# Graph-attention kernel: the normalised adjacency built inside the attention's last batch, and small buffers placed behind the large ones

## The reference

```python
# layer 0, per batch: attention with 4 heads whose queries come from a weighted adjacency product
A = abs(abs(sigmoid(diff) - 0.5) - 0.5) * 2.0
g = relu(einsum('bcn,bnm->bcm', fea, adj * (A + A.T) / 2) * para)
attn = softmax(einsum('bhnd,bhmd->bhnm', q, k) * scale);  out = attn @ v
x = layernorm(x + out)
# layer 1: graph convolution with the normalised adjacency, two linear layers with batch norms
A_norm = adj + eye(n)
deg = A_norm.sum(0) + A_norm.sum(1) - diagonal(A_norm)
dinv = rsqrt(deg)
A_hat = A_norm * dinv[:, None] * dinv[None, :]
agg = einsum('nm,bmd->bnd', A_hat, x)
h = relu(batchnorm(agg @ W1.T + b1));  out = batchnorm(h @ W2.T + b2)
x = layernorm(x + out)
```

## Time and profile before

| | us |
|---|---|
| median of 3 runs (lowest to highest) | 2815.95 (2815.73 to 2816.79) |
| the profiled execution's own time | 2817.06 |
| its span, first to last instruction | 2815.0 |
| TensorE busy | 2680.3 (95%) |
| VectorE busy | 1996.8 (71%) |
| ScalarE busy | 1662.9 (59%) |
| GpSimd busy | 1297.0 (46%) |

### The profile page before, as it was taken

The page is one execution under the profiler, slowest core; times in us unless marked ns, Lnnn a source line. Parts: engine busy times, 40 slices in busy tenths (PEclk is TensorE's granted clock), DMA queues, the critical chain, the costliest instruction groups (busy, mean ns, idle before and its releaser), DMA issues. The chain is left out here.

```text
span 2815.0 us, 39437 instructions
## 1 busy us (share of the span) xinstructions
PE 2680.3 (95%) x12436; PEld 1860.1 (66%) x12436; DVE 1996.8 (71%) x2875; ACT 1662.9 (59%) x2159; POOL 1297.0 (46%) x687
## 2 busy tenths in 40 slices
PE   8999999999999999999999999996899999989964
PEld 6566675656656566565666756663688888878854
DVE  7788796877868778797887968773533333348878
ACT  7666676675767667676666766754222222237768
POOL 5755757556575664757547575564100000000025
PEclk9999999999999999999999999998999999999985
DMA  4232222332222322223322223212122233215566
GB/s 139 77 96 75 75 78 75 92 95 75 67 86 69 102 90 67 71 78 97 93 72 75 78 75 97 75 53 105 60 90 89 104 104 104 90 32 192 180 242 250
DMA packets 126943, 272.01 MB, mean 97 GB/s; under 512 B 11952, under 2 KB 62128, under 8 KB 123312
## 3 DMA queue, kind: packets, MB, share of 16 engines
q1 hardware_dynamic: 126896, 271.42, 29.9%
HBM read 178.79 MB, written 62.98 MB: 86 GB/s over the span
## 5 line engine op out<-in xcount | busy, mean ns | idle before, releaser
L305 POOL TENSOR_TENSOR psum<-psum,probs 128x1024 f32<-128x1024 f32 x320 | 785.2, 2454 | 131.7 <-ACT probs L391 105.5
L391 ACT ACTIVATE probs<-sc_ps 128x1024 f32<-128x1024 f32 x512 | 507.6, 1023 | 403.2 <-PE sc_ps L852 400.2
L580 DVE TENSOR_REDUCE mx<-mx_ps 128x1 f32<-128x512 f32 x768 | 524.3, 690 | 255.2 <-PE mx_ps L821 252.6
L868 PE MATMUL pv_ps<-probs,v 128*64 128x512 f32 x2048 | 492.4, 604 | 0.0
L852 PE MATMUL sc_ps<-qa,ka 128*128 128x512 f32 x1024 | 387.3, 404 | 0.0
L852 PE MATMUL sc_ps<-qb,kb 128*128 128x512 f32 x1024 | 380.9, 395 | 1.6 <-DMA qb<-row 1.2
L821 PE MATMUL mx_ps<-ka,qa 128*128 128x512 f32 x768 | 314.2, 416 | 11.1 <-DVE mx L580 8.2
L868 PEld LDWEIGHTS pv_ps<-probs,v 128*64 128x64 f32 x2048 | 125.6, 136 | 220.8 <-issue 184.2
L1202 DVE TENSOR_TENSOR agg_lo<-ag_ps,agg_hi 128x1024 fp32r<-128x1024 f32 x32 | 39.2, 1224 | 312.3 <-ACT agg_hi L1129 312.3
L852 PEld LDWEIGHTS sc_ps<-qa,ka 128*128 128x128 f32 x1024 | 187.5, 188 | 106.9 <-issue 77.1
L821 PEld LDWEIGHTS mx_ps<-ka,qa 128*128 128x128 f32 x768 | 142.2, 187 | 161.6 <-issue 78.7
(11 more groups left out here) (198 smaller groups left out, 5524.5 us busy)
## 6 DMA issues: line engine op xcount, KB each, us to landing
adj_ring<-in_adj_dram SPq DMA_DIRECT2D x128, 512.0 KB, 3.6
pre_scratch<-pre SPq DMA_DIRECT2D x28, 1024.0 KB, 4.5
pre<-pre_scratch SPq DMA_DIRECT2D x28, 1024.0 KB, 5.0
x<-in_x_dram SPq DMA_DIRECT2D x16, 1024.0 KB, 5.5
kb<-ka SPq DMA_DIRECT2D x64, 256.0 KB, 3.2
res<-in_x_dram SPq DMA_DIRECT2D x16, 1024.0 KB, 5.5
x_scratch<-res SPq DMA_DIRECT2D x16, 1024.0 KB, 4.5
x1s<-x_scratch SPq DMA_DIRECT2D x16, 1024.0 KB, 7.5
```

The lines of the kernel that those rows point to most:

```text
L305: pool.tensor_tensor(psum[:, h % 2, :], probs[:, 0, :] if k == 1 else psum[:, h % 2, :], probs[:, k % PR, :], ALU.add).then_inc(s["pool_ad ...
L391: nc.scalar.activation(probs[:, i % PR, :], sc_ps[:, t % 2, :], ACT.Exp, scale=SCALE)\
L580: nc.vector.tensor_reduce(mx2[:, nh, n:n + 1], mx_ps[:, nh, :], AX.X, ALU.max)\
L868: ins = nc.tensor.matmul(pv_ps[nh * HD:(nh + 1) * HD, h % 2, :], v[:, i, h * HD:(h + 1) * HD], probs[:, i % PR, nh * BANK:(nh + 1) * BANK] ...
```

## The change

Part 1. The adjacency is made in the last batch of the attention. Its buffers `a_hi` and `a_lo` (and `pre`, `w2_hi`, `w2_lo`) are now made ahead of the attention, whose own buffers lie inside them as long as they are needed (`x32`, `neg_para` and `probs` in `pre`; `w_hi`, `x_hi`, `xT_hi`, `ka[0]` in `a_hi`). The slabs of `adj` are loaded in the last batch (SP), VectorE adds the identity and takes the diagonal after head 1's row (`augment`), ScalarE takes row sums in heads 2 and 3, TensorE the column sums in head 3 (`column_sums`), GpSimd `dinv` between its adds of head 3. ScalarE scales five slabs by `dinv`, VectorE three; TensorE transposes, ScalarE writes `a_hi` and VectorE `a_lo`, scaling by the other `dinv` on the way.

Part 2. `aggregate_layer` starts with the load of batch 0 in four pieces; the first product starts when the first piece is split, and the weights are transposed in its middle.

Part 3. `neg_half_b` and `neg_half_c` stand behind the large buffers. By the sizes, `a_hi`, `x1_hi`, `w1_hi`, `agg_hi`, `hid_hi` and their low parts all start on a multiple of 64 bytes now, as `w2_hi` does. In the attention `probs`, `ka[0]` and `qa[0]` start on one, while `v`, `kb`, `qb` and the other `ka` and `qa` are 32 bytes past.

Part 4. The last batch's result is normalised and stored in two halves.

```diff
+            def load_slabs(k):
+                if k == 0:
...
+                for t in SLABS[k]:
+                    sp.dma_start(slabs[t], slab_v[t]).then_inc(slabs_in[k], 16)
...
+            for k in range(2):
+                rows = slice(T // 2 * k, T // 2 * (k + 1))
+                wait(sp, s["res_done"], B + k)
+                sp.dma_start(x1_v[B - 1][:, rows, :], res[:, rows, :]).then_inc(s["x1_out"], 16)
...
+                        if last and (h, k) == (3, 1):
+                            pool.wait_ge(s["deg_done"], 1)
+                            pool.wait_ge(s["pool_added"], done + 1)
+                            pool.tensor_tensor(dinv[:, :], deg[:, :], neg_half[:, :], ALU.pow)\
+                                .then_inc(s["dinv_done"], 1)
...
+            def normal_adjacency(h, p):
+
+                if h == 2:
+                    for t in ((0,), (1, 2), (3, 4), (5, 6))[p]:
+                        row_sum(t)
+                if (h, p) == (3, 0):
+                    row_sum(7)
+                    col_copy()
+                if (h, p) == (3, 1):
+                    for t in ACT_SLABS[0:3]:
+                        scale_slab(t)
+                if (h, p) == (3, 2):
+                    for t in ACT_SLABS[3:]:
+                        scale_slab(t)
...
+            a_high(0)
             head_copy(B - 1, HEADS - 1)
+            a_high(1)
             den_copy(B - 1, HEADS - 1)
-            normalise(B - 1)
+            for m in range(2, 5):
+                a_high(m)
+            normalise(B - 1, range(0, T // 2))
+            normalise(B - 1, range(T // 2, T))
+            for m in range(5, T):
+                a_high(m)
...
+                    if h == 1 and last:
+                        augment(0)
+                        augment(1)
+                    if h == 2 and last:
+                        diagonal()
...
+                if last:
+                    degrees()
+                    scale_slabs(DVE_SLABS[0:2])
                 invert_sums(b, 2)
+                if last:
+                    scale_slabs(DVE_SLABS[2:])
...
+            a_low(0)
             add_last(B - 1, HEADS - 1)
+            a_low(1)
             invert_sums(B - 1, HEADS - 1)
             add_head(B - 1, HEADS - 1)
             row_stats(B - 1)
             moments(B - 1)
+            for m in range(2, T):
+                a_low(m)
...
+            def column_sums():
+                pe.wait_ge(s["augmented"], T)
+                pe.wait_ge(s["row_done"], 4 * B)
+                for t in range(T):
+                    for g in range(4):
+                        ins = nc.tensor.matmul(mx_ps[g * SG:(g + 1) * SG, 0, 0:SN], ones[:, :],
+                                               slabs[t][:, g * SN:(g + 1) * SN], start=t == 0, stop=t == T - 1)
+                ins.then_inc(s["colsum_ready"], 1)
...
+            def transpose_adjacency(m):
+                if m == 0:
+                    pe.wait_ge(s["scaled_act"], len(ACT_SLABS))
+                    pe.wait_ge(s["scaled_dve"], len(DVE_SLABS))
+                    pe.wait_ge(s["deg_done"], 1)
+                if m == 1:
+                    pe.wait_ge(s["exp_done"], 32 * B)
+                wait(pe, s["atl_done"], m - 2)
+                for t in range(T):
+                    ins = nc.tensor.transpose(at_tile(m)[:, t * P:(t + 1) * P], slabs[t][:, m * P:(m + 1) * P], ident[:, :])
+                ins.then_inc(s["at_ready"], 1)
...
-        neg_half = sb("neg_half_b", [P, T])
-        a_hi = sb("a_hi", [P, T, N], F32R)
-        a_lo = sb("a_lo", [P, T, N], F32R)
...
+        neg_half = sb("neg_half_b", [P, HT])
...
+            for k in range(PIECES):
+                rows = slice(PT * k, PT * (k + 1))
+                dve.wait_ge(piece_in[k], 16)
+                nc.vector.tensor_copy(x1_hi[:, rows, :], x1s[:, 0, rows, :]).then_inc(s["first_high"], 1)
+                dve.wait_ge(s["first_high"], k + 1)
+                nc.vector.tensor_tensor(x1_lo[:, rows, :], x1s[:, 0, rows, :], x1_hi[:, rows, :].bitcast(F32),
+                                        ALU.subtract).then_inc(s["first_low"], 1)
...
                 for m in range(T):
...
+                    pe.wait_ge(s["first_low"], m // PT + 1)
+                    if m == T // 2:
+                        transpose_weights()
...
-        neg_half = sb("neg_half_c", [P, OT])
         hid_hi = sb("hid_hi", [P, HT, N], F32R)
         hid_lo = sb("hid_lo", [P, HT, N], F32R)
...
+        neg_half = sb("neg_half_c", [P, OT])
```

More of the change, by code:

```diff
@@ L52, in row_moments, with attention_layer @@
     nc.vector.tensor_scalar(veps, part[:, 2, :], 0.25, EPS, ALU.mult, ALU.add).then_inc(veps_done, 1)
-def attention_layer(nc, x, adj, para, kv_w, sums, x1):
+def attention_layer(nc, x, adj, para, kv_w, sums, x1, a_hi, a_lo, late, late_hi, late_lo):
     B, N, C = x.shape
@@ L217, in body @@
                 sp.dma_start(res[:, :, :], res_v[b]).then_inc(s["res_in"], 16)
-                if not last:
+                if last:
+                    load_slabs(1)
+                else:
                     load_adj(b + 1, 0)
@@ L488, in body @@
                             normalise(b - 1, range(4 * p, 4 * p + 4))
-                        if not last:
+                        if last:
+                            normal_adjacency(h, p)
+                        else:
                             prepare(b + 1, h, p)
@@ L955, in body @@
                             values(b, h - 1, T - 1)
+                        if last and (h, p) == (3, 0):
+                            transpose_columns()
                 values(b, HEADS - 1, T - 2)
@@ L965, in _, with aggregate_layer @@
             over_batches(pe, B, body)
+            transpose_adjacency(1)
+            transpose_adjacency(2)
             sum_up(B - 1, HEADS - 1)
+            transpose_adjacency(3)
             transpose_sums(B - 1, HEADS - 1)
+            transpose_adjacency(4)
             transpose_back(B - 1, HEADS - 1)
-def aggregate_layer(nc, x1, adj, w1, b1, g1, be1, w2, ident, pre, w2_hi, w2_lo, scale1, shift1, pre1):
+            for m in range(5, T):
+                transpose_adjacency(m)
+def aggregate_layer(nc, x1, w1, b1, g1, be1, w2, ident, pre, w2_hi, w2_lo, scale1, shift1, pre1, a_hi, a_lo):
     B, N, C = x1.shape
@@ L1042, in _ @@
         def _(sp):
-            for t in range(T):
-                sp.dma_start(adjs[:, t, :], adj_v[:, t, :]).then_inc(adj_in[t], 16)
-                if t == 0:
-                    sp.dma_start(w1s, w1_v).then_inc(s["w1_in"], 16)
+            for k in range(PIECES):
+                rows = slice(PT * k, PT * (k + 1))
+                sp.dma_start(x1s[:, 0, rows, :], x1_v[0][:, rows, :]).then_inc(piece_in[k], 16)
+            sp.dma_start(w1s, w1_v).then_inc(s["w1_in"], 16)
             sp.dma_start(w2s, w2_v).then_inc(s["w2_in"], 16)
             def load(b, e):
-                wait(sp, s["x1l_done"], b - 1)
+                if isinstance(b, int) and b == 2:
+                    wait(sp, s["first_low"], PIECES)
+                else:
+                    wait(sp, s["x1l_done"], b - 2)
                 sp.dma_start(x1s[:, e, :, :], x1_v[b]).then_inc(x1_in[e], 16)
@@ L1685, in program @@
         y = pre[:, :, :, :].rearrange("p e t n -> p (e t n)").rearrange("p (r t c) -> p r t c", t=N // P, c=C)
+        with ExitStack() as adjacency:
+            a_hi = adjacency.enter_context(nc.sbuf_tensor("a_hi", [P, N // P, N], F32R))
+            a_lo = adjacency.enter_context(nc.sbuf_tensor("a_lo", [P, N // P, N], F32R))
+            attention_layer(nc, x, adj, para, kv_w, sums, x1, a_hi, a_lo, pre, w2_hi, w2_lo)
+            aggregate_layer(nc, x1, w1, b1, g1, be1, w2, ident, pre, w2_hi, w2_lo, scale1, shift1, pre1, a_hi, a_lo)
         x1_in = [ctx.enter_context(nc.semaphore(f"d_x1_in{r}")) for r in range(4)]
-        aggregate_layer(nc, x1, adj, w1, b1, g1, be1, w2, ident, pre, w2_hi, w2_lo, scale1, shift1, pre1)
         pre2 = ctx.enter_context(nc.sbuf_tensor("pre2", [P, O // P, B * (N // BANK), BANK], F32))
```

273 lines of the change are left out of this document (134 added, 139 removed).

## The result

| | before | changed |
|---|---|---|
| median, same chip, 4 runs each (lowest to highest) | 2815.84 (2814.68 to 2816.79) | 2788.59 (2787.34 to 2791.19) |
| profiled execution | 2817.06 | 2787.42 |
| its span | 2815.0 | 2785.6 |

The ratio is 0.9905, 95% interval 0.9893 to 0.9917: 27.25 us faster, where 24.9 were forecast. A later set of four runs of the same kernel had a median of 2791.07 beside 2816.68 for before (25.6 less). All eight runs together lie between 2787.34 and 2792.96, a wider scatter than that of before; the experiments come back to it.

A forecast was written before the change was run, and what follows sets the result against it. TensorE, busy 95% of the span, was taken as the bound, with a 56.5 us chain between engines before the aggregate layer. -19.5 - 5.4 = -24.9 us from 2817.06 gave 2792.2, or 2791.1 as a median; range 2785 to 2801.

The forecast's parts named there:

- The start of the first product: Aggregate layer: the first product starts at 1965.4 instead of 1987.38, 22.0 us earlier.
- The head's addition: Last attention batch: stall, column sums and transposes added on TensorE make the last head's addition 9.7 us late.
- The stall behind `augment`: Last batch: TensorE's third maxima product waits 2.1 us behind VectorE's 16 small instructions; bounds nothing to 3.3.
- GpSimd's cover: Last batch: the last add ends at 1938.6, TensorE reaches `sum_up` at 1940.9, leaving 2.3 us of cover.
- The row: Profile row on VectorE beside GpSimd: VectorE pays and the sum stays; the skill's rule instead adds up to 1.4 us.
- The first product: Aggregate layer: the weights' 16 transposes now inside it add 2.1 us, the lower clock 0.4 (0 to 1.5).
- The output layer's step: Output layer: with operands placed in step, 768 matmuls gain 7 ns each, 5.4 us.
- keeps its step: Rival: part 3 does nothing for the output layer's matmuls, total 2796.5 us; chance 0.27.
- The values: Attention's value matmuls, `probs` and `v` now placed differently: nothing taken; at 7 ns a pair it would be 7.2 us.
- The rivals at 2798 and at 2832: Attention's values pay for operand places: 7.2 us, total 2798, chance 0.08; or 40 ns a pair, 2832, chance 0.03.
- The rival in which the last batch takes more: Late GpSimd adds or exponentials push `sum_up`: 2797 us with the output layer's gain, 2802 without; chance 0.10.
- More gained: Rival: first piece lands sooner and TensorE has no stall behind `augment`, total 2787 to 2784 us; chance 0.02.

The follow-up runs named there:

- after_again: The changed kernel run once more as it is, nothing altered; median 2791.07 us, ratio 0.9906 to the kernel before.
- e1: The changed kernel with `neg_half_c` put back in front of `hid_hi` and `hid_lo`; median 2794.79 us, ratio 0.9929 to the kernel before.
- e3: The changed kernel with `neg_half_b` put ahead of `x1_hi` and `w1_hi` in the aggregate layer; median 2801.83 us, ratio 0.9951 to the kernel before.
- e2: The changed kernel with a 32-byte spacer ahead of `w2_hi`, shifting moving data and weights alike; median 2791.64 us, one of four executions taking 7322.22 us.
- e4: The kernel before with only `neg_half_c` moved behind `hid_hi` and `hid_lo`; median 2811.33 us, ratio 0.9983 to the kernel before.
- e10: The changed kernel with the 16 small instructions of `augment` spread over several places in the last batch; median 2785.80 us, ratio 0.9890 to the kernel before.
- e5: The changed kernel with both steps of `augment` moved into VectorE's idle gaps in the last batch; median 2793.01 us, ratio 0.9917 to the kernel before.
- e9: The changed kernel with six slabs scaled by VectorE and two by ScalarE, instead of three and five; median 2798.23 us, ratio 0.9934 to the kernel before.

## Why the prediction was right, step by step

- **The start of the first product**: 22.0 us earlier forecast, 26.0 in the profile. The mechanism held; the 4.0 are made of these. The head's addition was to be 9.7 late and was, from the last batch's start and without the landing of `qb`, 8.7 late: stall 2.26 (2.1 forecast), column sums 3.59 (4.6), transposes of the columns 0.2 (0.3), tile 0 0.97 (1.0), tiles 1 and 2 0.6 (0.8), tiles 3 and 4 0.7 (0.9), and 0.3 in small pieces. The one term of this sum that was off by more than a few tenths is the column sums: I priced four products at the 0.57 of the earlier trace rows, which holds the turn from one kind of work to the next; 32 in a row take 0.112 each. The moments to the block took 11.08 (11.2 forecast), the block to the first product 3.89 (4.4). 0.9 us came in the fifteen batches before, whose period fell from 119.54 to 119.47 (119.49 in after_again), which no term had; 1.4 is the landing of `qb`. The profile of after_again, which waits for `qb` as that of before does, comes nearer: last values 1939.06 (1939 forecast), the head's addition 1944.18 (1944), block 1960.67 (1961), first product 1964.63 (1965.4). A part of that is luck: the lower clock behind the stall, 1.6 us there and in no term, stands where the column sums were priced 1.0 too high and the tiles 0.4.
- **The stall behind `augment`** was in the sum at 2.1, but without the clock behind it: 1.5 us more in half of the profiles. I had said "one idle stretch of about 2 us", and it was; I had not asked what it does to the granted clock. It is one of the costs that can put the median of eight runs, 2790.3, 3 us above the best one and near the 2791.1 forecast; only two of the eight have a profile, so its share in the others isn't shown.
- **GpSimd's cover** was to be 2.3 us. `add_last` ended at 1937.14 and `sum_up` began at 1937.71: 0.57 left. The five additions took 1.15 us more beside the scalings, and `sum_up` came 3.2 us earlier than forecast where the start of the additions came 2.65 earlier. The cover held, and by less than I thought. The row won on the sum, since nothing of it reached the path, but not on the mechanism: both engines pay, in turns. The Trainium skill ("SBUF — State Buffer", "Who interferes with whom") gives the pair of ports that the two engines share to whichever instruction issues first, for its whole length, and has the other wait; the prediction took only one of these two cases from it. The traces agree with both. The scaling that started first lasted 0.75 us and the addition behind it 2.88 instead of 2.36; the scaling that started second lasted 2.88 and ended 0.55 us after the addition, and the next addition lasted 2.71. In the changed kernel the three scalings take 2.8 us more than three times 0.75, the five additions 1.15 more than before: VectorE has the larger share.
- **The first product** was to lose 2.5 us to the weights' transposes and the clock; it lost 1.6 in the first profile and 3.1 in after_again (26.71 us long), where the granted clock over it is 0.88 instead of 0.94.
- **The output layer's step** was the term with the least behind it: one layer of each kind, 5.4 us forecast, 4.9 measured, and shown four ways: undone (e1, +5.0), made in the other layer (e3, +10.4), both operands shifted (e2, none), alone in the kernel before (e4, -4.8). So the rival "keeps its step" at 2796.5 falls. The step is 13 ns beyond 512 columns at 2.4 GHz when the places agree and 20 when they don't; by the Trainium skill's 2.5 ns ("TensorE: Matmul & The Clock Gate", "Wait — 56ns, not 53.3ns?") neither e1, e3 nor e4 would have moved.
- **The values** did not pay for their operands' places: 2048 of them have a mean duration of 604 ns and 492.4 us in all in both kernels. The rivals at 2798 and at 2832 fall with it. Why this form is immune was not tried.
- **The rival in which the last batch takes more** falls too: it needed `sum_up` pushed by three to six microseconds of other work, and the last values end at 1935.88 and 1939.06 in the two profiles, where 1939 was forecast. *More gained* named 2787 to 2784, with no stall behind `augment`; the stall was there, and it took e10 to come that low.

The sum, -24.9, missed the first comparison's -27.25 by 2.4 us and the second's -25.6 by 0.7.

What stays open: why the batches' period fell by 0.07 us; what decides in an execution whether the clock falls behind a wait of 2.26 us; and how far places other than 32 bytes apart behave alike, as only 0 and 32 modulo 64 were run. Two pieces of the change, the weights transposed in the middle of the first product and the normalisation and store in two halves, were not undone by themselves.

## What to carry to other kernels

Lay out the two operands of a long stream of fp32r matmuls of 512 columns alike: a buffer of 32 bytes put behind a large one instead of ahead of it was worth 5 us in this kernel, and with it in the wrong layer it costs 10. Before filling a gap of VectorE, look at what GpSimd does in that gap: a small instruction with both inputs in SBUF, or a scaling, that starts behind one of its long additions waits for that addition's end. And price a stall of TensorE at its length plus the time behind it at the lower clock, and look at several executions for it: a wait of 2.3 us cost up to 3.8.

## What the runs showed of the hardware that I had not expected

- VectorE's 128x128 additions with both inputs in SBUF, 0.28 us alone, took up to 2.45 us beside GpSimd's additions of 2.4 (e5), and its scalings of 128x1024 took 2.8 instead of 0.75 (e9). The first ended 0.15 us after GpSimd's instruction, a scaling 0.55 after it. VectorE's instructions with one input in PSUM were not held: eight of `add_head`, beside an addition from 1931.46 on in the changed kernel, lasted 0.27 to 0.28 us each.
- GpSimd lost less than VectorE did: its five additions took 12.20 us with no scaling beside them, 13.35 with three, 13.97 with six.
- Either operand 32 bytes off the other, moving data or weights, costs the same: 0.233 and 0.234 us a step instead of 0.227.
- The same stretch of program behind the same wait ran at a granted clock of 1.00 in four profiles and 0.72 in four.
